# A planner's table of VectorE durations, and how far ahead steps of the head may stand

## The chip, the cores and the metric

The kernel runs on one core of a Trainium2 chip. The metric is the device time of one execution in microseconds (us). It has no loop on the chip: every instruction of the five engines is written out by a program that first makes a plan, and the plan alone fixes the order on each engine. TensorE is called PE here and in the rows, VectorE DVE, ScalarE ACT, GpSimd POOL, and SyncE, which issues the transfers, SP.

## What is computed

Sixteen sequences of 1024 tokens with 256 channels go through half a gated FFN, causal attention with 16 heads and rotary embedding, and the same FFN again, each on a layer norm without weights:

```
def ffn(x):                      # x_prev is x moved by one token, zero at the start
    xr = mu_r * x + (1 - mu_r) * x_prev
    xk = mu_k * x + (1 - mu_k) * x_prev
    r = sigmoid(xr @ W_r.T)
    return r * (square(relu(xk @ W_k.T)) @ W_v.T)

x = x + 0.5 * ffn(layernorm(x))
x = x + softmax(causal(rope(q) @ rope(k).T / 4)) @ v @ W_proj + b_proj    # q, k, v of layernorm(x)
x = x + 0.5 * ffn(layernorm(x))
```

## The kernel before

**Slots.** Time is cut into slots, one for each block of scores (`score_slot`). A score is one matmul of L938 (128 keys by up to 512 queries of one head), and 48 of them make up a group of four heads, so a batch has four groups and 192 slots; the whole program has 3072 scores. ACT takes the exponential of each score (L1064), and in bursts PE multiplies them with the values (L969). A slot has also a *maximum*: another matmul of queries by keys (L948), whose rows DVE reduces (L1175 for blocks on the diagonal, L1178 for the others) to the maxima that a later group's exponentials subtract. Three PSUM banks (`NM`) hold such blocks, so PE can't write the fourth before DVE has taken the first. The slots before the first of the second group's scores are the *head*: slot -120 is the start, the first 16 maxima stand from slot -53 (`HALF_MAX`), the others from -33 (`REST_MAX`), the first 16 scores (called S1 to S16 here) from -25, the 17th (S17) at slot 16. From there on the number of a slot and of its score agree.

**Background steps.** All else fills the gaps between scores and maxima: the FFN steps `f_...` of one chunk of 256 tokens (index p runs over 128 chunks in the order of `self.ffn`; p = 0 to 3 is batch 0, p = 4 to 7 batch 1), the layer norm and value steps `a_...`, the queries and keys `r_...`, the output projection `p_P`. On PE a background matmul of 128x256 in float32 is one of four of a step and shows as two records. The steps that matter here:

- `f_dif` on POOL (L1330) takes the difference to the token before. `f_k0`, `f_k1` on DVE (L1200) and `f_r0`, `f_r1` (L1206) make the mixed inputs from two SBUF tiles, `dif_sb` and `fxn_sb`. Then come `f_K` on PE (L1022), `f_R` (L1025), `f_V` (L1028), `f_u` on DVE (L1212, one operand in PSUM) and `f_xadd` on POOL (L1335).
- `r_QK` on PE (L1034), four transfers `r_swap` (L846), `r_cos` on POOL (L1348), `r_sin` and `r_add` on DVE (L1229, L1233, two SBUF tiles each), then `r_hi`, `r_rest`, `r_mid`, `r_low` split the result into three bfloat16 parts, and SP sends them to the rows that scores and maxima read (L861 for a whole group, `rows0` to `rows5`; L873 for the first half of the first group, `part0` to `part5`).
- `y_mul` on POOL (L1359), then `p_P` on PE (L1015) and `xp` on DVE.

**The planner.** `describe` gives each step a start slot t (`release`), and `step` turns it into the first slot in which it may stand. Two procedures place the steps. `place_early` handles the slots before 48 (`SWITCH`) by credits; it doesn't read the table of durations. From slot 48 on `place`, `fill` and `unit` keep a clock for each engine and read `TAKES`: name: (ns until the engine can begin the next instruction, ns until others see the result). A step is placed when its inputs are seen by that clock, and on DVE only where its first number fits before the next maximum.

Of the kernel before, what the change touches and what calls it, by code (L numbers as in the profile page):

```python
# [62 lines left out]
SWITCH = 48  # L63
# [22 lines left out]
class Plan:  # L86


    TAKES = {"f_st0": (335, 470), "f_st1": (600, 760), "f_rstd": (1600, 1700), "f_x0": (490, 645), "f_x1": (490, 645), "f_T": (440, 640),
             "f_xn": (477, 645), "f_dif": (1270, 1330), "f_k0": (397, 530), "f_k1": (397, 530), "f_r0": (397, 530), "f_r1": (397, 530),  # L90
             "f_relu": (477, 665), "f_sq": (500, 675), "f_tanh": (477, 645), "f_u": (600, 735), "f_xadd": (1222, 1330),
             "a_st0": (335, 470), "a_st1": (600, 760), "a_rstd": (1600, 1700), "a_x0": (490, 645), "a_x1": (490, 645), "a_T": (440, 640),
             "a_xn": (477, 645), "a_vc": (477, 645), "a_bias": (1222, 1330), "r_b0": (356, 530), "r_b1": (356, 530), "r_swap": (240, 7000),
             "r_cos": (1350, 1700), "r_sin": (700, 840), "r_add": (603, 740), "r_hi": (519, 680), "r_rest": (1170, 1500), "r_mid": (519, 680),
             "r_low": (1170, 1500), "store": (60, 5000), "load": (60, 7000), "h_fin": (700, 900), "h_T": (130, 400), "h_copy": (156, 330),
             "h_rows": (240, 2500), "m_fin": (900, 1000), "m_T": (130, 400), "m_copy": (157, 330), "m_rows": (60, 3000),
             "y_copy": (477, 645), "y_out": (120, 8000), "y_recip": (159, 300), "y_back": (60, 4500), "y_in": (120, 9000),
# [6 lines left out]
    HEARD_PE = 200  # L104
    UNIT = 4 * CH / GHZ
    TICK = 900
    EARLY = 60

    def __init__(self, nb):
        self.nb = nb  # L110
# [12 lines left out]
    def step(self, engine, name, i, cost, start, *after):  # L123

        turn = 0 if name[0] in "myh" else 1 if name[:4] in ("rows", "part") else 2
        early = start - self.EARLY if turn == 2 else start
        if name == "a_vc":
            early = max(early, (i // NCH - 1) * BSLOTS + PV_AT + 1)
        self.steps[name, i] = [engine, cost, (turn, start), early, [(n, k, lag) for n, k, lag in after if k >= 0]]
# [1288 lines left out]
```

## Time and profile before

| | us |
|---|---|
| median of 3 runs (3065.30 to 3073.12) | 3072.01 |
| the profiled execution | 3072.22 |
| its span, first to last instruction | 3070.50 |
| from the start to the first maximum's matmul | 89.18 |
| to S1 | 113.60 |
| to S17 | 158.90 |
| to the 49th, 97th, 145th, 193rd score | 190.79, 231.63, 272.61, 317.11 |
| two batches in the middle (192 scores each) | 181.60, 183.30 |

In the profile PE is busy for 95% of the span, DVE for 82%, ACT 72%, POOL 52%. In the first 100 us PE is busy for 66.77 us, from 100 to 200 us for 84.40. A busy PE isn't a PE at its peak, since the ends of matmuls are modelled. The chain that ended last runs over PE for 70% of the span and over DVE for 17%. The granted TensorE clock is 0.987 over the span.

### The profile page before, as it was taken

Reading aid. Unit: us, or ns where it says so; the run is one execution under the profiler, and the core shown is the slowest. Engines: PE = TensorE matmul, PEld = TensorE weight load, DVE = VectorE, ACT = ScalarE, POOL = GpSimd, SP = SyncE. Lnnn points to the kernel's source line nnn. Section 1 sums busy time; section 2 is a strip of 40 time slices with the busy share of each in tenths; the row PEclk is TensorE's granted clock in tenths of the full one; section 3 lists DMA queues with packets and bytes.
Section 4 is the critical chain, followed back from the end, with each engine's and each line's share of the span. In section 5 each row is a group of like instructions: output and inputs, shape, how many; then the busy total and the mean of one; then the engine's idle time right before and its main releaser. Section 6 shows DMA issues by size and latency. Waiting matters only on the chain.

```text
span 3070.5 us, 56204 instructions
## 1 busy us (share of the span) xinstructions
PE 2916.8 (95%) x18245; PEld 1710.7 (56%) x18245; DVE 2513.0 (82%) x7302; ACT 2197.9 (72%) x4802; POOL 1588.8 (52%) x2190
## 2 busy tenths in 40 slices
PE   6799999999999999999999999999999999999997
PEld 5545555655555555555555555565555655555444
DVE  3888888888888888888888888888888888888852
ACT  4467677777777777777777777777777777777663
POOL 5555544655555455555555555555455555555222
PEclk9899999999999999999999999999999999999998
DMA  3334443433433434443433433443343443443411
GB/s 100 67 67 78 77 94 68 97 78 74 95 73 86 84 74 90 79 98 60 101 78 71 92 77 88 81 88 77 75 105 60 98 78 71 95 79 86 78 44 35
DMA packets 202585, 245.49 MB, mean 80 GB/s; under 512 B 68405, under 2 KB 104245, under 8 KB 202293
## 3 DMA queue, kind: packets, MB, share of 16 engines
q1 hardware_dynamic: 202293, 241.90, 38.1%
q8 instruction: 146, 2.39, 0.4%
q14 instruction: 146, 1.20, 0.2%
HBM read 53.48 MB, written 51.38 MB: 34 GB/s over the span
## 4 chain that ended last, share of the span: by engine, by line
PE 70%; DVE 17%; issue 4%; ACT 4%; POOL 3%; DMA 1%; SPq 1%; POOLq 0%; DVEq 0%; ACTq 0%
PE ps_y L969 14%; PE ps_s L938 13%; PE ps_m L948 12%; PE ps_d L1022 7%; PE ps_d L1025 6%; PE ps_d L1028 5%; PE ps_d L1034 5%; DVE ps_m L1175 4%; DVE mx_sb L1178 3%; PE ps_d L1015 3%; PE ps_d L1038 3%; DVE ka_sb L1200 3%; PE ps_d L976 2%; ACT pt_sb L1064 2%; DVE dif_sb L1206 1%
## 5 line engine op out<-in xcount | busy, mean ns | idle before, releaser
L1064 ACT ACTIVATE pt_sb<-ps_s 128x512 f32<-128x512 f32 (+1 forms) x2532 | 1219.4, 492 | 483.7 <-PE ps_s L938 456.7
L1175 DVE CUSTOM_DVE_ANT_0 ps_m<-ps_m,mask_sb 128x128 f32<-128x128 f32 (+3 forms) x2048 | 993.1, 498 | 298.7 <-PE ps_m L948 282.5
L948 PE MATMUL ps_m<-kr_sb,qr_sb 96*128 96x512 bf16 (+3 forms) x3072 | 1002.3, 329 | 39.0 <-DVE mx_sb L1175 29.8
L938 PE MATMUL ps_s<-qr_sb,kr_sb 99*128 99x512 bf16 (+1 forms) x3039 | 996.5, 330 | 24.6 <-ACT pt_sb L1064 9.3
L1178 DVE TENSOR_REDUCE mx_sb<-ps_m 128x1 f32<-128x512 f32 x1024 | 699.0, 683 | 99.4 <-PE ps_m L948 92.3
L1307 POOL TENSOR_SCALAR_AFFINE_SELECT pt_sb<-pt_sb 128x512 f32<-128x512 f32 x384 | 255.6, 666 | 503.3 <-ACT pt_sb L1064 503.1
L948 PEld LDWEIGHTS ps_m<-kr_sb,qr_sb 96*128 96x128 bf16 x3072 | 301.9, 98 | 365.4 <-DVE mx_sb L1175 74.6
L969 PE MATMUL ps_y<-pt_sb,v_sb 128*32 128x512 f32 (+2 forms) x5120 | 494.5, 495 | 3.3 <-POOL pt_sb L1307 3.0
L938 PEld LDWEIGHTS ps_s<-qr_sb,kr_sb 99*128 99x128 bf16 x3039 | 293.4, 97 | 328.0 <-issue 134.0
L1064 ACT ACTIVATE pn_sb<-ps_s 128x384 f32<-128x384 f32 x507 | 244.7, 493 | 244.9 <-PE ps_s L938 243.4
L1022 PE MATMUL ps_d<-ka_sb,wk_sb 128*128 128x256 f32 x992 | 307.2, 398 | 29.4 <-DVE ka_sb L1200 28.7
L1025 PE MATMUL ps_d<-wr_sb,dif_sb 128*128 128x256 f32 x1024 | 307.5, 387 | 4.4 <-DVE dif_sb L1206 4.3
L1034 PE MATMUL ps_d<-axn_sb,wqk_sb 128*128 128x256 f32 x1024 | 305.3, 383 | 4.4 <-ACT axn_sb L1104 3.8
L1028 PE MATMUL ps_d<-wv_sb,ka_sb 128*128 128x256 f32 x992 | 296.4, 383 | 0.0
L1175 DVE DVE_READ_ACCUMULATOR2_ANT mx_sb<- 128x1 f32 x2048 | 285.9, 140 | 0.0
L969 PEld LDWEIGHTS ps_y<-pt_sb,v_sb 128*32 128x32 f32 x5120 | 141.6, 110 | 237.2 <-issue 210.6
L1335 POOL TENSOR_TENSOR x_sb<-x_sb,dif_sb 128x512 f32<-128x512 f32 x128 | 179.2, 1400 | 182.1 <-DVE dif_sb L1212 181.9
L1351 POOL TENSOR_TENSOR qb_sb<-qb_sb,part_sb 128x512 f32<-128x512 f32 x124 | 147.0, 1186 | 181.9 <-ACT part_sb L1123 181.6
L1022 PEld LDWEIGHTS ps_d<-ka_sb,wk_sb 128*128 128x128 f32 x992 | 178.2, 198 | 79.4 <-issue 40.1
L1034 PEld LDWEIGHTS ps_d<-axn_sb,wqk_sb 128*128 128x128 f32 x1024 | 180.6, 190 | 49.1 <-issue 3.7
L1200 DVE SCALAR_TENSOR_TENSOR ka_sb<-dif_sb,muk_sb,fxn_sb 128x256 f32<-128x256 f32 x248 | 200.5, 816 | 8.5 <-POOL dif_sb L1330 8.4
L1025 PEld LDWEIGHTS ps_d<-wr_sb,dif_sb 128*128 128x128 f32 x1024 | 178.9, 192 | 45.9 <-issue 6.7
(113 smaller groups left out, 3934.9 us busy)
## 6 DMA issues: line engine op xcount, KB each, us to landing
kr_sb<-part_sb SPq DMA_DIRECT2D x378, 128.0 KB, 4.5
qr_sb<-part_sb SPq DMA_DIRECT2D x378, 128.0 KB, 4.8
y_way<-yt_sb SPq DMA_DIRECT2D x128, 256.0 KB, 2.2
sw_sb<-qb_sb SPq DMA_DIRECT2D x496, 64.0 KB, 2.0
x_sb<-x SPq DMA_DIRECT2D x64, 256.0 KB, 3.9
yn_sb<-y_way SPq DMA_DIRECT2D x64, 256.0 KB
den_sb<-r_way SPq DMA_DIRECT2D x64, 256.0 KB
out<-x_sb SPq DMA_DIRECT2D x64, 256.0 KB, 2.4
```

Of the source, the lines that this page charges most:

```text
L938: eng.matmul(score_bank(slot)[:, 0:width], kr_sb[0:KR + NP, n % RS, j, kb * P:(kb + 1) * P], qr_sb[0:KR + NP, n % RS, j, q0:q0 + width], s ...
L948: eng.matmul(ps_m[:, u % NM, 0:width], qr_sb[0:KR, n % RS, j, i * P:(i + 1) * P], kr_sb[0:KR, n % RS, j, piece * QC:piece * QC + width], s ...
L969: pv_j = eng.matmul(ps_y[32 * j:32 * j + 32, QC - width:QC], v_sb[:, b % 2, kb, col:col + 32], buffer[:, j, column:column + width], start= ...
L1022: mm = eng.matmul(ps[:, rows], wk_sb[:, cc, cols], key_of(i)[:, cc, :], start=(cc == 0), stop=(cc == CC - 1))
L1025: mm = eng.matmul(ps[:, rows], dif_sb[:, i % 2, cc, cols], wr_sb[:, cc, :], start=(cc == 0), stop=(cc == CC - 1))
L1028: mm = eng.matmul(ps[:, rows], key_of(i)[:, cc, cols], wv_sb[:, cc, :], start=(cc == 0), stop=(cc == CC - 1))
L1034: mm = eng.matmul(ps[:, rows], wqk_sb[:, cc, w0:w0 + P], axn_sb[:, c, cc, :], start=(cc == 0), stop=(cc == CC - 1))
L1064: eng.activation(buffer[:, j, column:column + width], score_bank(slot)[:, 0:width], ACT.Exp, scale=SCALE).then_inc(exped, 1)
L1175: eng.tensor_tensor_reduce(ps_m[:, u % NM, 0:width], ps_m[:, u % NM, 0:width], mask_sb[:, m0:m0 + width], 1.0, -3e38, ALU.add, ALU.max, be ...
L1178: eng.tensor_reduce(best, ps_m[:, u % NM, 0:width], mybir.AxisListType.X, ALU.max).then_inc(max_taken, 1)
L1200: eng.scalar_tensor_tensor(out=key_of(i)[:, cc, :], in0=dif_sb[:, i % 2, cc, :], scalar=muk_sb[:, cc:cc + 1], in1=fxn_sb[:, i % 2, cc, 0:C ...
L1307: eng.affine_select(out=diag, in_=diag, compare_op=ALU.is_ge, fill=0.0, base=0, pattern=[[0, G], [1, P]], channel_multiplier=-1).then_inc( ...
```

## The change

```diff
     TAKES = {...
-             "f_xn": (477, 645), "f_dif": (1270, 1330), "f_k0": (397, 530), "f_k1": (397, 530), "f_r0": (397, 530), "f_r1": (397, 530),
+             "f_xn": (477, 645), "f_dif": (1270, 1330), "f_k0": (760, 900), "f_k1": (760, 900), "f_r0": (560, 700), "f_r1": (560, 700),
...
-             "r_cos": (1350, 1700), "r_sin": (700, 840), "r_add": (603, 740), "r_hi": (519, 680), "r_rest": (1170, 1500), "r_mid": (519, 680),
+             "r_cos": (1350, 1700), "r_sin": (820, 960), "r_add": (700, 840), "r_hi": (519, 680), "r_rest": (1170, 1500), "r_mid": (519, 680),
...
-    EARLY = 60
+    EARLY_HEAD, EARLY = 16, 60
...
-        early = start - self.EARLY if turn == 2 else start
+        early = min(start - self.EARLY_HEAD, max(start - self.EARLY, SWITCH)) if turn == 2 else start
```

No instruction is added, taken away or made different; instructions stand in another order. A background step (`turn == 2`) could stand up to 60 slots ahead of its start slot. Now a step whose start is before slot 64 may stand 16 ahead at most, one with a start between 64 and 108 not before slot 48, and later ones 60 ahead as before. The six names in the table are the DVE steps with two SBUF operands; the table acts from slot 48 on.

**The head, on PE**, from the projections of batch 0's last chunks to the first maxima (L1034 queries and keys, L1038 values, L976 a transpose, L1007 the bias, L1022, L1025 and L1028 the FFN of batch 1's first chunk). Before:

```order
25 L1034 MATMUL ps_d<-axn_sb,wqk_sb 128x256 x4
26 L1038 MATMUL ps_d<-wvv_sb,axn_sb 128x256 x8
27 L1034 MATMUL ps_d<-axn_sb,wqk_sb 128x256 x8
28 L976 MATMUL ps_d<-id_sb,dif_sb 128x128 x4
29 L1007 MATMUL ps_d<-wp_sb,yt_sb 128x256 x2
30 L1022 MATMUL ps_d<-ka_sb,wk_sb 128x256 x4
31 L1025 MATMUL ps_d<-wr_sb,dif_sb 128x256 x4
32 L1028 MATMUL ps_d<-wv_sb,ka_sb 128x256 x4
33 L948 MATMUL ps_m<-kr_sb,qr_sb 128x512 x2
34 L1034 MATMUL ps_d<-axn_sb,wqk_sb 128x256 x3
```

Now:

```order
25 L1034 MATMUL ps_d<-axn_sb,wqk_sb 128x256 x4
26 L1038 MATMUL ps_d<-wvv_sb,axn_sb 128x256 x8
27 L948 MATMUL ps_m<-kr_sb,qr_sb 128x512 x4
28 L948 MATMUL ps_m<-kr_sb,qr_sb 128x128 x4
29 L948 MATMUL ps_m<-kr_sb,qr_sb 128x384 x4
30 L948 MATMUL ps_m<-kr_sb,qr_sb 128x256 x4
31 L1034 MATMUL ps_d<-axn_sb,wqk_sb 128x256 x4
32 L997 MATMUL ps_d<-idb_sb,hp_sb 48x128
```

The 22 background matmuls and the transpose between the values and the first maximum stand later; the first sixteen maxima follow each other.

**Behind the head, on PE**, around the 103rd to 106th score, where work arrives that stood in the head. Before:

```order
378 L938 MATMUL ps_s<-qr_sb,kr_sb 128x384
379 L948 MATMUL ps_m<-kr_sb,qr_sb 128x256
380 L938 MATMUL ps_s<-qr_sb,kr_sb 128x384
381 L948 MATMUL ps_m<-kr_sb,qr_sb 128x512
382 L938 MATMUL ps_s<-qr_sb,kr_sb 128x256
383 L948 MATMUL ps_m<-kr_sb,qr_sb 128x256
```

Now:

```order
379 L938 MATMUL ps_s<-qr_sb,kr_sb 128x384
380 L948 MATMUL ps_m<-kr_sb,qr_sb 128x256
381 L1038 MATMUL ps_d<-wvv_sb,axn_sb 128x256
382 L938 MATMUL ps_s<-qr_sb,kr_sb 128x384
383 L948 MATMUL ps_m<-kr_sb,qr_sb 128x512
384 L1022 MATMUL ps_d<-ka_sb,wk_sb 128x256
385 L938 MATMUL ps_s<-qr_sb,kr_sb 128x256
386 L948 MATMUL ps_m<-kr_sb,qr_sb 128x256
387 L1022 MATMUL ps_d<-ka_sb,wk_sb 128x256
```

Each slot has a background matmul now where it had none.

**In the middle of the run, on DVE**, around the 1061st score. Before:

```order
2571 L1200 SCALAR_TENSOR_TENSOR ka_sb<-dif_sb,muk_sb,fxn_sb 128x256
2572 L1175 ISA ps_m,mx_sb<-ps_m,mask_sb 128x384
2573 L1175 ISA mx_sb 128x1
2574 L1175 ISA ps_m,mx_sb<-ps_m,mask_sb 128x256
2575 L1175 ISA mx_sb 128x1
2576 L1229 TENSOR_TENSOR sw_sb<-sw_sb,sin_sb 128x512
2577 L1200 SCALAR_TENSOR_TENSOR ka_sb<-dif_sb,muk_sb,fxn_sb 128x256
2578 L1233 TENSOR_TENSOR qb_sb<-qb_sb,sw_sb 128x512
2579 L1206 SCALAR_TENSOR_TENSOR dif_sb<-dif_sb,mur_sb,fxn_sb 128x256 x2
2580 L1175 ISA ps_m,mx_sb<-ps_m,mask_sb 128x256
```

Now:

```order
2570 L1175 ISA ps_m,mx_sb<-ps_m,mask_sb 128x384
2571 L1175 ISA mx_sb 128x1
2572 L1175 ISA ps_m,mx_sb<-ps_m,mask_sb 128x256
2573 L1175 ISA mx_sb 128x1
2574 L1200 SCALAR_TENSOR_TENSOR ka_sb<-dif_sb,muk_sb,fxn_sb 128x256 x2
2575 L1206 SCALAR_TENSOR_TENSOR dif_sb<-dif_sb,mur_sb,fxn_sb 128x256
2576 L1175 ISA ps_m,mx_sb<-ps_m,mask_sb 128x256
2577 L1175 ISA mx_sb 128x1
2578 L1206 SCALAR_TENSOR_TENSOR dif_sb<-dif_sb,mur_sb,fxn_sb 128x256
```

Five steps stood between two maxima; now there are three, and the rotary steps aren't in this gap.

## Rows read from the trace of the kernel before

**Rows 1.** The page: busy us (share of the span) xinstructions of each engine.

```profile
PE 2916.8 (95%) x18245; PEld 1710.7 (56%) x18245; DVE 2513.0 (82%) x7302; ACT 2197.9 (72%) x4802; POOL 1588.8 (52%) x2190
```

**Rows 2.** Waits of PE from 576 to 2640 us: us in total, times, longest.

```profile
PE ps_m L948 <- DVE mx_sb L1175: 13.6, 17, 1.0
PE ps_d L1022 <- DVE ka_sb L1200: 12.5, 16, 1.1
PE ps_d L1015 <- POOL yn_sb L1359: 9.0, 11, 1.5
PE ps_d L1025 <- DVE dif_sb L1206: 4.3, 11, 0.5
```

**Rows 3.** DVE's groups by form: xcount | busy us, mean ns | idle before, releaser.

```profile
L1178 DVE TENSOR_REDUCE mx_sb<-ps_m 128x1 f32<-128x512 f32 x1024 | 699.0, 683 | 99.4 <-PE ps_m L948 92.3
...
L1200 DVE SCALAR_TENSOR_TENSOR ka_sb<-dif_sb,muk_sb,fxn_sb 128x256 f32<-128x256 f32 x248 | 200.5, 816 | 8.5 <-POOL dif_sb L1330 8.4
L1206 DVE SCALAR_TENSOR_TENSOR dif_sb<-dif_sb,mur_sb,fxn_sb 128x256 f32<-128x256 f32 x256 | 152.9, 610 | 0.0
...
L1229 DVE TENSOR_TENSOR sw_sb<-sw_sb,sin_sb 128x512 f32<-128x512 f32 x124 | 110.7, 892 | 8.5 <-DMA sw_sb<-qb_sb 8.5
...
L1233 DVE TENSOR_TENSOR qb_sb<-qb_sb,sw_sb 128x512 f32<-128x512 f32 x124 | 95.2, 768 | 4.9 <-POOL qb_sb L1348 3.2
```

**Rows 4.** Timeline of DVE around the 1061st score: start us, us, instruction.

```profile
1138.57 1.46 DVE L1200 SCALAR_TENSOR_TENSOR ka_sb<-dif_sb,muk_sb,fxn_sb 128x256 f32<-128x256 f32 x1
...
1140.81 0.91 DVE L1229 TENSOR_TENSOR sw_sb<-sw_sb,sin_sb 128x512 f32<-128x512 f32 x1
...
1142.42 1.76 DVE L1233 TENSOR_TENSOR qb_sb<-qb_sb,sw_sb 128x512 f32<-128x512 f32 x1
1144.11 0.87 DVE L1206 SCALAR_TENSOR_TENSOR dif_sb<-dif_sb,mur_sb,fxn_sb 128x256 f32<-128x256 f32 x2
```

**Rows 5.** Timeline of POOL in the same stretch.

```profile
1142.19 1.44 POOL L1335 TENSOR_TENSOR x_sb<-x_sb,dif_sb 128x512 f32<-128x512 f32 x1
```

**Rows 6.** Timeline of PE right behind it.

```profile
1145.43 0.39 PE L948 MATMUL ps_m<-kr_sb,qr_sb 96*128 96x512 bf16 x1 [1.01 <-DVE mx_sb L1175]
```

**Rows 7.** Timeline of PE in the head.

```profile
61.96 3.62 PE L1038 MATMUL ps_d<-wvv_sb,axn_sb 128*128 128x256 f32 x16
...
81.27 3.75 PE L1022 MATMUL ps_d<-ka_sb,wk_sb 128*128 128x256 f32 x8 [4.94 <-DVE ka_sb L1200]
...
89.18 0.60 PE L948 MATMUL ps_m<-kr_sb,qr_sb 96*128 96x512 bf16 x2
```

**Rows 8.** Timeline of DVE in the head.

```profile
70.13 0.69 DVE L1233 TENSOR_TENSOR yn_sb<-yn_sb 128x512 f32<-128x512 f32 x1 [1.16 <-POOL yn_sb L1348]
...
101.54 0.84 DVE L1249 TENSOR_SCALAR hp_sb<-mx_sb 128x16 bf16<-128x16 f32 x1
```

**Rows 9.** Timeline of SP in the head: the last `part` transfer and the last of `rows5`.

```profile
59.39 0.59 SPq L873 DMA_DIRECT2D qr_sb<-part_sb  x1
...
84.07 0.59 SPq L861 DMA_DIRECT2D qr_sb<-part_sb  x1
```

**Rows 10.** The page's transfers: xcount, KB each, median us from issue to landing.

```profile
kr_sb<-part_sb SPq DMA_DIRECT2D x378, 128.0 KB, 4.5
```

**Rows 11.** Two stretches, of L938 alone: us, PE busy (xscores), PEld busy, clock, DMA, GB/s.

```profile
89.18:113.60 24.42, 0.00 (x0) 0.10 (x1) 0.93 0.17 43
113.60:158.90 45.30, 4.99 (x16) 1.57 (x16) 0.89 0.46 70
```

**Rows 12.** Stretches of 48 scores, of `ps_d` alone: us, PE busy (xrecords), PEld, DVE, ACT, clock.

```profile
231.63:272.61 40.98, 13.74 (x51) 8.40 (x51) 0.68 (x1) 4.29 (x9) 1.00 0.45 77
...
407.30:453.60 46.30, 26.46 (x96) 15.72 (x95) 1.35 (x2) 7.40 (x14) 1.00 0.49 98
...
634.30:678.50 44.20, 22.31 (x84) 13.28 (x83) 1.35 (x2) 6.32 (x12) 1.00 0.43 79
2828.50:2861.70 33.20, 0.22 (x1) 0.12 (x1) 0.00 (x0) 0.45 (x2) 1.00 0.47 82
```

## The prediction

> **What bounds the kernel now.** I read the page first, then the waits of PE in the middle of the run, then the lines and the timeline of DVE, last the head. PE is busy for 95% of the span and DVE for 82% [rows 1]: PE is the bound through most of the run, with DVE close behind. The work is fixed, so a new order can win only what PE waits for, and what the head loses before the first scores. In the middle, over 2064 us, PE waits 13.6 us for a maximum's bank that DVE hasn't freed, 12.5 us for `f_k`, 4.3 us for `f_r` and 9.0 us for `y_mul` [rows 2]. That is 39 us in about eleven batches: the ceiling for the middle.
>
> The causes are in DVE's rows. A step of L1200 takes 816 ns on the mean where the planner reckons with 397, one of L1206 610 (397), L1229 892 (700), L1233 768 (603) [rows 3]. Consecutive DVE records overlap a little, so the new entries, 760, 560, 820 and 700, are near the mean pace. But the mean hides two kinds. One step of L1200 took 1.46 us [rows 4]. In the pile of five steps that the last excerpt of the order shows, L1233 took 1.76 us while POOL ran L1335, and two steps of L1206 behind it took 0.87 us together [rows 4, 5]. By the old table this pile takes 2.5 us (700 + 397 + 603 + 2 x 397 ns); by the trace it lasts from 1140.81 to about 1144.9, 4.1 us [rows 4]. PE then waited 1.01 us for the bank [rows 6].
>
> **The head: first maxima and first scores.** Until PE has made the values, which end at 61.96 + 3.62 = 65.6 us [rows 7], its order is the same. Before, 22 background matmuls stood ahead of the first maximum. Twelve are the FFN of batch 1's first chunk, and PE waited 4.94 us for their `f_k` alone; the first maximum came at 89.18 [rows 7]. The rows it reads were not the cause: their last transfer was issued at 59.39 [rows 9] and takes some 4.5 us [rows 10], so they lay there at 64.5. Now PE can make it at 65.6, and DVE, after `r_add` of the last chunk (70.13 + 0.69 [rows 8]), takes it at 70.8. The sixteen first maxima took from 89.18 to 101.54 with other steps between [rows 7, 8], 12.4 us, so at most as long now: done by 83.2. The next maxima need the whole group's rows. Their last transfer was issued at 84.07 [rows 9]; with 0.59 us of issue and 4.5 to land that is 89.2. Now no `load` and no `r_swap` stands between these issues, and ACT and POOL no longer have batch 1's FFN between the parts of the last chunk. I take 4 us for it: 85. Eight maxima at some 0.76 us (683 ns by L1178 [rows 3]; diagonal ones take a little more) and one `r_sin` of 0.9 bring S1 to about 91.5, where it stood at 113.60 [rows 11]. **Gain 22 us**; 18 if the rows land as late as before; 24 at best.
>
> From S1 to S17, 45.30 us [rows 11], the order holds 33 background matmuls both times, and 25 DVE steps for 24: **0**. From S17 to the 49th score it holds 20 for 16, and 13 DVE steps for 6. Seven steps of 0.6 to 0.9 us are 5 us if DVE binds there, 1.8 us of matmuls if PE does: **cost 3.5 us**.
>
> **Behind the head: what was moved comes back.** Up to the 49th score, 33 fewer background matmuls are done; from there to the 145th score there are now 73 for 41, and by the 193rd both orders are level within one matmul. A background matmul is two records of 0.226 us (3.62 us for 16 [rows 7]), 0.45 us, if PE has no room. It has some: a stretch of 48 scores with 51 records took 40.98 us and one with 96 took 46.30 us at the same place of a batch, 5.3 us for 45 records, 0.24 us for each background matmul [rows 12]. 32 matmuls cost 7.7 us at that price and 14.4 us at the full one. Eleven more DVE steps come with them where DVE has little room, so I take **9 us**.
>
> From the 193rd to the 577th score the new order has 22 fewer (277 for 299), at 0.24 us a **gain of 5 us**. They come back between scores 2689 and 2881 (148 for 128). Sixteen of them fill a stretch that had none; it took 33.20 us with one record, and the like stretch with 84 took 44.20 [rows 12], 0.13 us a record, so 4.2 us, and 1 us for the rest: **cost 5 us**. The last chunks behind the last score stand as before: 0.
>
> Sum outside the middle: -22 + 0 + 3.5 + 9 - 5 + 5 = **-9.5 us**.
>
> **The middle, eleven batches.** The new table makes piles smaller: no gap has more than four steps where six were possible. In the gap shown, three steps remain for five. Of 13.6 us for banks I let two thirds go: -9. The projection stood one slot behind its `y_mul` in two of eight cases and stands ten slots or more behind in all of them now: -9 [rows 2]. `f_R` has fewer close followers: -2 of 4.3. `f_K` is the weak place: before, it stood in the slot right behind `f_k1` in 5 of 16 cases, now in 8. The planner has more time in that slot, but a step beside POOL takes twice what it has: 0 of 12.5. Last, one more slot in each batch has no background matmul at all, at about 0.25 us: +3. The sum is **-17 us**; bounds are -36 (all of rows 2, less 3) and +15 (`f_K`'s waits grow with its close followers and with POOL, and nothing else goes).
>
> The profiled execution took 3072.2 us around its span of 3070.5, as the median of 3072.0. 3072.2 - 9.5 - 17 = 3045.7: I predict **3046 us**.
>
> **A rule of the skill.** L1206 ran at 0.44 us each with POOL out of the way, and L1233 took 1.76 us beside L1335 [rows 4, 5]. The Trainium skill, SBUF — State Buffer, "Who interferes with whom", says that a VectorE instruction with two SBUF inputs contends with a GpSimd instruction that reads SBUF. The trace agrees. By that rule no single number is right for these steps, which speaks against this change; it is the first rival.
>
> **Rivals.** *Slower: the new order makes more steps meet POOL.* `f_k0` follows `f_dif` on POOL at once, and POOL's next step starts then too. Eight of 16 `f_K` stand in the slot behind `f_k1`, 64 in the run. A pair that meets POOL takes up to twice 1.46 us [rows 4], where the table has 1.5 for both: 1.4 us late. If half of these 64 meet it, that is 45 us for `f_K`, less 12.5 that is already paid, and longer DVE steps eat the gain on the other waits. Then the middle costs some 30 us: 3072.2 - 9.5 + 30 = **3093 us**. It decides once more than about a third of the close pairs meet POOL. For it: in the mean of L1200, 816 ns, (816 - 440)/(1460 - 440), some four steps in ten are slow already. Against it: the steps that met POOL now cost only 12.5 us.
>
> *The same: the head's gain is paid back in full.* The first maxima wait for the group's rows as before (-18), the moved matmuls cost 0.45 us each behind the head (32 at 14.4 us, after the 5 us of DVE steps before them), the late ones cost 9 (20 at 0.45) where 5 are gained ahead, and the middle gives 2: 3072.2 - 18 + 5 + 14.4 - 5 + 9 - 2 = **3076 us**. For it: PE is at 95%, and work moved out of a stretch where it idles must be done where it doesn't.
>
> *Faster still:* all waits of rows 2 but the 3 us of empty slots go, and S1 comes at 89.5: 3072.2 - 11.5 - 36 = **3025 us**.
>
> *The change doesn't do what it says* in the head: the procedure that places the head doesn't read the table, and the limit of sixteen slots could bind on nothing. The order excludes this; 66 steps leave the head.
>
> **How the numbers follow.** A measurement can tell about 0.3% (9 us) from no change. Chances: forecast (3034 to 3055) 0.42, faster still 0.18, the same 0.23, slower 0.17. "Faster by over 0.3%" is under 3062.8: the first two and a little of the third, 0.63; within 0.3% 0.21; slower 0.16. The range takes in the bounds of the middle with the head's at their likely values, and leaves out the far part of the slower rival: 3019 to 3082.
>
> **What would show it.** Right if S1 stands at 89 to 95 us, S17 at 134 to 141, the 49th score near 172 and the 193rd near 307 (317.11 before), and if two batches in the middle take about 363 us for 366. The wait of L1015 for `y_mul` should be gone, that of L948 for DVE a third. Wrong if the first maximum still comes after 75 us, if the 193rd score is no earlier than before, or if the mean of L1200 rises well above 816 ns and the wait of L1022 doubles.

## The result, and the profile of the changed kernel

The change makes the kernel slower: 3113.70 us (median of 4 runs, 3111.85 to 3117.54) against 3070.81 us (4 runs, 3065.30 to 3073.12), a ratio of 1.0138 with an interval of 1.0124 to 1.0153. The prediction of 3046 us (range 3019 to 3082) is wrong, in its sign too: it put PE's wait for the row transfers at nothing, and that wait is 83.3 us. The profiled execution has a span of 3111.9 us, 41.4 more than before.

The start of each numbered score or maximum, read from the timeline of PE (us):

| | before | after | difference |
|---|---|---|---|
| first maximum | 89.18 | 64.30 | -24.9 |
| S1 | 113.60 | 87.8 | -25.8 |
| S17 | 158.90 | 138.8 | -20.1 |
| 49th score | 190.79 | 171.7 | -19.1 |
| 97th | 231.63 | 214.6 | -17.0 |
| 145th | 272.61 | 274.7 | +2.1 |
| 193rd | 317.11 | 317.7 | +0.6 |
| 577th | 678.5 | 665.4 | -13.1 |
| 2689th | 2691.0 | 2731.4 | +40.3 |
| 2881st | 2861.7 | 2914.7 | +53.0 |
| the last | 3008.1 | 3052.7 | +44.5 |

So the head came as forecast, and the middle went the other way: 53.4 us lost in eleven batches where 17 were to be won. The page answers [rows 1]; PE, DVE, ACT and POOL are each busy within 7.5 us of what they were:

```profile
PE 2924.2 (94%) x18245; PEld 1722.0 (55%) x18245; DVE 2507.9 (81%) x7302; ACT 2200.9 (71%) x4802; POOL 1581.4 (51%) x2190
```

The waits of PE from 576 to 2700 us answer [rows 2] (what is waited for: us in total, times, longest):

```profile
PE ps_m L948 <- DMA qr_sb<-part_sb: 65.6, 11, 6.9
PE ps_s L938 <- ACT pt_sb L1064: 10.7, 33, 0.5
PE ps_d L1025 <- DVE dif_sb L1206: 0.2, 1, 0.2
```

All four waits that the prediction counted are gone, three of them whole. A wait that the rows of before don't have has taken their place: the maximum's matmul waits for the transfer of the rows it reads, once in each batch from the fifth on (batches are counted from 0, so 4 to 15), and once in batch 1. Over the whole run it is

```profile
PE ps_m L948 <- DMA qr_sb<-part_sb: 83.3, 13, 12.3
```

Twelve of these stand at the first maximum of a batch's first group (groups 16, 20, ... 60; group 4b is the first of batch b) and take 5.1 to 6.9 us each; one of 12.3 us stands at group 4. In the timeline of PE (start us, us, instruction, idle before) the one at group 24:

```profile
1163.44 0.38 PE L938 MATMUL ps_s<-qr_sb,kr_sb 99*128 99x512 bf16 x1
1170.05 0.61 PE L948 MATMUL ps_m<-kr_sb,qr_sb 96*128 96x512 bf16 x1 [6.23 <-DMA qr_sb<-part_sb]
1170.45 1.06 PE L1038 MATMUL ps_d<-wvv_sb,axn_sb 128*128 128x256 f32 x2
```

and SP's timeline just ahead of it:

```profile
1154.84 0.65 SPq L838 DMA_DIRECT2D out<-x_sb  x1
1155.58 0.61 SPq L891 DMA_DIRECT2D dcol_sb<-yt_sb  x1
1156.23 0.50 SPq L892 DMA_DIRECT2D y_way<-yt_sb  x1
1156.77 0.56 SPq L861 DMA_DIRECT2D kr_sb<-part_sb  x1
1157.38 0.60 SPq L861 DMA_DIRECT2D qr_sb<-part_sb  x1
1158.15 0.65 SPq L906 DMA_DIRECT2D yn_sb<-y_way  x1
1158.85 0.64 SPq L909 DMA_DIRECT2D den_sb<-r_way  x1
1159.53 0.61 SPq L861 DMA_DIRECT2D kr_sb<-part_sb  x1
1160.18 0.61 SPq L861 DMA_DIRECT2D qr_sb<-part_sb  x1
```

The last row transfer is issued at 1160.18. Before, that transfer of the same group was issued at 1154.24 for a maximum at 1168.65. Landing takes longer too. Minimum, median and maximum from issue to landing of the row transfers (L861), for all twelve of this group before, and for the last five that write `qr_sb` now:

```profile
DMA to landing us min/median/max: 3.4/4.4/5.7
DMA to landing us min/median/max: 4.6/5.0/9.8
```

The 9.8 is that of the last one: 1160.18 + 9.8 = 1170.0, where the matmul starts.

VectorE's two-operand steps answer [rows 3] (count, busy us, mean ns, idle before):

```profile
L1200 DVE SCALAR_TENSOR_TENSOR ka_sb<-dif_sb,muk_sb,fxn_sb 128x256 f32<-128x256 f32 x248 | 182.3, 746 | 5.7 <-POOL dif_sb L1330 5.7
L1206 DVE SCALAR_TENSOR_TENSOR dif_sb<-dif_sb,mur_sb,fxn_sb 128x256 f32<-128x256 f32 x256 | 151.9, 602 | 0.0
...
L1229 DVE TENSOR_TENSOR sw_sb<-sw_sb,sin_sb 128x512 f32<-128x512 f32 x124 | 122.0, 984 | 5.0 <-DMA sw_sb<-qb_sb 5.0
...
L1233 DVE TENSOR_TENSOR qb_sb<-qb_sb,sw_sb 128x512 f32<-128x512 f32 x124 | 97.4, 785 | 13.5 <-POOL qb_sb L1348 10.9
```

The mean of L1200 fell from 816 to 746 ns and that of L1229 rose from 892 to 984. The busy time of the four is 553.6 us for 559.3.

### The profile page after: what moved, and what is told of

The parts are those of the page before. It is cut to its first block, busy times and chain, and to the rows that moved or that the text cites. A ratio compares the mean times of both kernels' runs of the same rounds, so it can differ in the third digit from the quotient of the medians.

```text
span 3111.9 us, 56208 instructions
## 1 busy us (share of the span) xinstructions
PE 2924.2 (94%) x18245; PEld 1722.0 (55%) x18245; DVE 2507.9 (81%) x7302; ACT 2200.9 (71%) x4802; POOL 1581.4 (51%) x2190
## 4 chain that ended last, share of the span: by engine, by line
PE 76%; DVE 8%; SPq 6%; DMA 5%; ACT 3%; issue 2%; POOL 1%; POOLq 0%; DVEq 0%; ACTq 0%
PE ps_y L969 15%; PE ps_s L938 14%; PE ps_m L948 13%; PE ps_d L1025 7%; PE ps_d L1034 6%; PE ps_d L1028 6%; PE ps_d L1022 6%; DMA qr_sb<-part_sb 4%; PE ps_d L1015 3%; SPq L861 3%; DVE ps_m L1175 3%; PE ps_d L1038 3%; PE ps_d L976 3%; DVE mx_sb L1178 2%; ACT pt_sb L1064 2%
## 5 line engine op out<-in xcount | busy, mean ns | idle before, releaser
L948 PE MATMUL ps_m<-kr_sb,qr_sb 96*128 96x512 bf16 (+3 forms) x3072 | 1014.2, 332 | 114.8 <-DMA qr_sb<-part_sb 83.3
L938 PE MATMUL ps_s<-qr_sb,kr_sb 99*128 99x512 bf16 (+1 forms) x3039 | 1003.6, 331 | 28.3 <-ACT pt_sb L1064 17.7
L938 PEld LDWEIGHTS ps_s<-qr_sb,kr_sb 99*128 99x128 bf16 x3039 | 294.9, 97 | 341.8 <-issue 135.6
L1025 PE MATMUL ps_d<-wr_sb,dif_sb 128*128 128x256 f32 x1024 | 319.3, 399 | 0.6 <-DVE dif_sb L1206 0.6
L1034 PE MATMUL ps_d<-axn_sb,wqk_sb 128*128 128x256 f32 x1024 | 314.2, 392 | 3.8 <-ACT axn_sb L1104 3.8
L1022 PE MATMUL ps_d<-ka_sb,wk_sb 128*128 128x256 f32 x992 | 301.9, 388 | 8.5 <-DVE ka_sb L1200 7.8
L1028 PE MATMUL ps_d<-wv_sb,ka_sb 128*128 128x256 f32 x992 | 297.7, 384 | 0.0
L1335 POOL TENSOR_TENSOR x_sb<-x_sb,dif_sb 128x512 f32<-128x512 f32 x128 | 171.3, 1338 | 101.4 <-DVE dif_sb L1212 100.9
L1025 PEld LDWEIGHTS ps_d<-wr_sb,dif_sb 128*128 128x128 f32 x1024 | 188.3, 201 | 44.2 <-issue 10.0
L1307 POOL TENSOR_SCALAR_AFFINE_SELECT pn_sb<-pn_sb 128x512 f32<-128x512 f32 x128 | 82.0, 640 | 254.5 <-ACT pn_sb L1064 254.5
L1034 PEld LDWEIGHTS ps_d<-axn_sb,wqk_sb 128*128 128x128 f32 x1024 | 178.9, 194 | 46.9 <-issue 3.9
L1022 PEld LDWEIGHTS ps_d<-ka_sb,wk_sb 128*128 128x128 f32 x992 | 172.3, 193 | 57.3 <-issue 9.6
```

The costliest lines, as they stand in the source:

```text
L938: eng.matmul(score_bank(slot)[:, 0:width], kr_sb[0:KR + NP, n % RS, j, kb * P:(kb + 1) * P], qr_sb[0:KR + NP, n % RS, j, q0:q0 + width], s ...
L948: eng.matmul(ps_m[:, u % NM, 0:width], qr_sb[0:KR, n % RS, j, i * P:(i + 1) * P], kr_sb[0:KR, n % RS, j, piece * QC:piece * QC + width], s ...
L1022: mm = eng.matmul(ps[:, rows], wk_sb[:, cc, cols], key_of(i)[:, cc, :], start=(cc == 0), stop=(cc == CC - 1))
L1025: mm = eng.matmul(ps[:, rows], dif_sb[:, i % 2, cc, cols], wr_sb[:, cc, :], start=(cc == 0), stop=(cc == CC - 1))
L1028: mm = eng.matmul(ps[:, rows], key_of(i)[:, cc, cols], wv_sb[:, cc, :], start=(cc == 0), stop=(cc == CC - 1))
L1034: mm = eng.matmul(ps[:, rows], wqk_sb[:, cc, w0:w0 + P], axn_sb[:, c, cc, :], start=(cc == 0), stop=(cc == CC - 1))
```

## The experiments

**The theory.** The new table makes the planner place the background chain of a batch later: layer norm, queries and keys, rotary steps, row transfers. By the plans, the last of the row steps (`rows5`) stood 15 slots ahead of the first maximum of each batch's first group, and from group 16 on it now stands 5 ahead; the `r_low` that it sends stood 34 ahead and now 12. The 5 slots don't cover issue and landing, and PE waits. The head's limit does the same to group 4 alone. **The rivals:** the loss is the price of the work moved out of the head (*paid back*), or VectorE's steps meet POOL more often (*POOL*). "Rows ahead" below is the distance in the plan from `rows5` to that maximum, at group 4 and at groups 16, 20, ... 60 (middle); the wait is that of PE for `qr_sb<-part_sb` at the first maxima of the groups, without single waits under 0.9 us; the batch is the mean of ten batches between the 577th and the 2497th score.

| kernel | rows ahead, group 4 / middle | waits, us (times) | a batch, us | median, us |
|---|---|---|---|---|
| before | 15 / 15 | 0 | 183.1 | 3071 to 3074 |
| changed | 4 / 5 | 83.3 (13) | 187.8 | 3113.7 |
| table alone | 15 / 5 | 70.8 (12) | 187.6 | 3115.2 |
| head alone | 1 / 15 | 10.6 (1) | 183.1 | 3070.3 |
| rotary entries old | 4 / 15 | 12.5 (1) | 181.3 | 3040.2 |
| rows issued earlier (than planned) | 4 / 5 | 12.0 (1) | 181.7 | 3041.1 |
| margin 1000 | 4 / 12 | 11.5 (1) | 180.2 | 3026.2 |
| slack 500 | 11 / 15 | 3.9 (1) | 181.5 | 3043.7 |
| rotary entries alone | 1 / 1 | 109.6 (14) | 191.8 | 3171.2 |
| rows issued earlier, limit 28 | 12 / 5 | 0.9 (1) | 181.7 | 3035.1 |
| margin 1000, limit 28 | 12 / 12 | 0 | 180.2 | 3024.1 |
| margin 1000, limit at the first maximum | 15 / 12 | 0 | 180.2 | 3018.9 |
| old table, limit 28 | 15 / 15 | 0 | 183.2 | 3071.7 |
| old table, margin 1000 | 15 / 12, but 8 at group 28 and 1 at group 32 | 11.7 (2) | 184.7 | 3106.5 |

**The two halves apart.** The table alone:

```diff
-        early = min(start - self.EARLY_HEAD, max(start - self.EARLY, SWITCH)) if turn == 2 else start
+        early = start - self.EARLY if turn == 2 else start
```

> The table alone; the head stands as before the change. Theory 'late rows': the new table puts the row transfers of each batch's first group only 5 slots ahead of the maximum that reads them (15 before), so twelve waits of about 6.2 us for them (groups 16 to 60) stay, each followed by some 5 us at half the TensorE clock; group 4 has its rows 15 slots ahead, so its wait of 12.3 us is not there, and neither is the head's gain of 19 us. From the 49th score to the 577th it should run as before the change (488 us), from there as the changed kernel. That gives 3113.7 + 19 - 12.3 - 2 + 11 or so: 3120 to 3132 us, and waits of L948 for the rows of some 71 us in all. Rival 'paid back' (the loss is the price of the work moved out of the head): 3050 to 3065, since nothing is moved. Rival 'POOL' (the new order makes VectorE's two-operand steps meet GpSimd): 3110 to 3130 as well, but with the loss in waits of PE for DVE, not for the rows.

Measured: 3115.24 us, ratio 1.0139 [1.0120, 1.0159]; twelve waits, 70.8 us, none at group 4, as expected. The time is 5 us under the 3120 to 3132 expected: from the 49th to the 577th score it takes 473.5 us, where the 487.7 of before had been reckoned with. The head alone is the kernel before with

```diff
-        early = start - self.EARLY if turn == 2 else start
+        early = min(start - 16, max(start - self.EARLY, SWITCH)) if turn == 2 else start
```

> The sixteen-slot limit alone, with the old table. Late rows: in the middle the rows stand 15 slots ahead again, so no wait for them there and 183 us for a batch as before; at group 4 they stand 1 slot ahead (4 in the changed kernel), so that wait is 12 to 18 us. Against the kernel before: -19 us at the 49th score, about +22 to the 145th, -10 to the 577th, then level: 3060 to 3070 us. Rival 'paid back': 3105 to 3115, with the loss spread over the run. Rival 'POOL': about 3050 to 3060, and nothing in it speaks for the table's part.

Measured: 3070.34 us, ratio 0.9989 [0.9978, 1.0001]. The expectation was 3060 to 3070, with a wait of 12 to 18 us at group 4; it is 10.6. So the whole loss is the table's, and it lies in the waits. The rival *paid back* doesn't make the loss, but with the old table it holds for the head: 19.0 us ahead at the 49th score, 0.4 behind at the 577th, 10.6 of it in the wait at group 4.

**The cause itself.** In the changed kernel only SP's order is edited; the orders of PE, DVE, ACT and POOL are word for word the same:

```diff
-            for slot in slots:
-                for name, i in plan.at["SP"].get(slot, ()):
+            line = [step for slot in slots for step in plan.at["SP"].get(slot, ())]
+            for g in range(NG, nb * NG, NG):
+                for k in (4, 5):
+                    line.remove((f"rows{k}", g))
+                    line.insert(line.index((f"rows{k - 1}", g)) + 1, (f"rows{k}", g))
+            if True:
+                for name, i in line:
```

> The changed kernel with every order as it is but SP's: from group 4 on, the last two of the six row steps of each batch's first group are issued right behind the fourth, ahead of a store and the transfers of the attention's result that stood between. The orders of PE, DVE, ACT and POOL are the changed kernel's, word for word. Late rows: the last row transfer is issued some 3.4 us earlier and has fewer transfers ahead of it in the queue, so the wait of 6.2 us falls to 0 to 3 us, and with it most of the 5 us at half clock: 3113.7 less 40 to 95 us, 3020 to 3075. Rivals 'POOL' and 'paid back': no VectorE, GpSimd or TensorE instruction stands elsewhere, so 3105 to 3120.

Measured: 3041.08 us, ratio to the kernel before 0.9900 [0.9882, 0.9918]; 73 us less than the changed kernel. SP's timeline at the same place (line numbers from here on are 5 higher in this kernel: L866 is L861):

```profile
1145.61 0.60 SPq L866 DMA_DIRECT2D kr_sb<-part_sb  x1
1146.25 0.59 SPq L866 DMA_DIRECT2D qr_sb<-part_sb  x1
1146.89 0.59 SPq L843 DMA_DIRECT2D out<-x_sb  x1
1147.58 0.61 SPq L896 DMA_DIRECT2D dcol_sb<-yt_sb  x1
1148.23 0.49 SPq L897 DMA_DIRECT2D y_way<-yt_sb  x1
1148.88 1.00 SPq L911 DMA_DIRECT2D yn_sb<-y_way  x1
```

the row transfers' landing there, the maximum, which doesn't wait, and PE's waits from 576 to 2700 us:

```profile
DMA to landing us min/median/max: 3.4/5.3/6.3
```

```profile
1153.24 0.38 PE L953 MATMUL ps_m<-kr_sb,qr_sb 96*128 96x512 bf16 x1
```

```profile
PE ps_s L943 <- ACT pt_sb L1069: 11.6, 36, 0.5
PE ps_m L953 <- DVE mx_sb L1180: 10.9, 13, 1.6
PE ps_m L953 <- DVE mx_sb L1183: 3.4, 11, 0.3
PE ps_m L953 <- DMA qr_sb<-part_sb: 1.1, 2, 0.9
```

The store and the transfers of the attention's result, four of them of 256 KB, now stand behind the last rows. From the end of `r_low` to the last issue it takes 6.1 us (1140.17 to 1146.25) where it took 9.6 (1150.58 to 1160.18), and the slowest landing 6.3 for 9.8: 7 us in all, for a wait of 6.2. This settles the cause. Not one instruction of VectorE or GpSimd stands elsewhere, which leaves neither rival for these waits.

**The same by way of the plan.** Rotary entries old:

```diff
-             "r_cos": (1350, 1700), "r_sin": (820, 960), "r_add": (700, 840), "r_hi": (519, 680), "r_rest": (1170, 1500), "r_mid": (519, 680),
+             "r_cos": (1350, 1700), "r_sin": (700, 840), "r_add": (603, 740), "r_hi": (519, 680), "r_rest": (1170, 1500), "r_mid": (519, 680),
```

> The changed kernel with r_sin and r_add at their old entries (700, 840 and 603, 740); f_k and f_r keep the new ones. Late rows: in this plan the rows of the middle groups stand 15 slots ahead of their maxima, those of group 4 still 4. So 12 waits of L948 for rows go (71 us, and some 2.5 us behind each at half clock), the one of 12.3 us at group 4 stays: 3113.7 - 71 - 30 = about 3013 if nothing else moves, 3010 to 3050 with the waits for DVE that may come back. Rival 'POOL': f_k and f_r are 504 of the 752 steps with a new entry and keep it, so most of the loss stays: 3090 to 3115.

Measured: 3040.20 us, ratio 0.9894 [0.9878, 0.9911]; only group 4's wait is left. The reverse is the changed kernel with

```diff
-             "f_xn": (477, 645), "f_dif": (1270, 1330), "f_k0": (760, 900), "f_k1": (760, 900), "f_r0": (560, 700), "f_r1": (560, 700),
+             "f_xn": (477, 645), "f_dif": (1270, 1330), "f_k0": (397, 530), "f_k1": (397, 530), "f_r0": (397, 530), "f_r1": (397, 530),
```

> The changed kernel with f_k and f_r at their old entries, r_sin and r_add at the new ones: by the plan the row steps stand only 1 slot ahead of their maxima at group 4 and at the middle groups, the last part (r_low) 1 slot. Late rows, as a dose the other way: a wait of about 12 us at each of the thirteen groups (4 slots ahead cost 12.3 at group 4, 5 ahead 6.2 in the middle; r_low to maximum took 19.5 us with 5 slots ahead, some 10 to 12 of it the row steps and their landing), so 160 us of waits: 3160 to 3230. Rival 'POOL': fewer steps have new entries and the piles are more as before the change, so 3060 to 3115.

Measured: 3171.15 us (2 runs), ratio 1.0321 [1.0300, 1.0342]. So the two rotary entries by themselves are what makes the rows late, 1 slot ahead of the maximum; with the entries of `f_k` and `f_r` added it is 5. The waits are 7.6 to 9.4 us in the middle, not the 12 expected: at group 24 it took 13.5 us from the end of `r_low` to the maximum, where it took 19.5 in the changed kernel, and the slowest row transfer landed after 8.3 us for 9.8. The direction was right, the size of a wait per slot was not.

The planner's margin for SP, which it adds to a step's inputs, 1000 for 1500 ns:

```diff
-    MARGIN = {"PE": 0, "ACT": 200, "DVE": 400, "POOL": 400, "SP": 1500}
+    MARGIN = {"PE": 0, "ACT": 200, "DVE": 400, "POOL": 400, "SP": 1000}
```

> The changed kernel with the planner's margin for SP at 1000 ns instead of 1500: the row steps of each batch's first group stand 12 slots ahead of their maximum in the middle (5 in the changed kernel, 15 before the change), at group 4 still 4. Late rows, as a dose: 7 slots of some 0.95 us are 6.6 us, just the wait, so 0 to 1.5 us of it remain at each of the twelve groups; group 4 keeps its 12 us. With the undisturbed pace seen where the rows were issued earlier (181.75 us for 192 scores): 3040, 3030 to 3055. Rival 'POOL', or anything else in the order of VectorE: the new table is unchanged, so 3095 to 3120.

Measured: 3026.19 us, ratio 0.9850 [0.9835, 0.9865], below the 3030 to 3055 expected. Twelve slots are enough. The margin gives more than the rows' wait: the eleven batches from the 577th to the 2689th score take 1981.5 us, 18 less than with the rows issued earlier, and only 6 of these are waits of PE (19.4 us of all kinds for 25.3). The rest was not taken further. And VectorE's slack, how far past the next maximum a step's first number may reach:

```diff
-    SLACK = {"ACT": 250, "DVE": 400, "POOL": 1300, "SP": 300}
+    SLACK = {"ACT": 250, "DVE": 500, "POOL": 1300, "SP": 300}
```

> The changed kernel with all new entries and VectorE's slack (how far past the next maximum a step's first number may reach) at 500 ns instead of 400: rows 15 slots ahead in the middle, 11 at group 4. Late rows: no wait in the middle, 0 to 3 us at group 4: 3025, 3015 to 3045. Rival 'POOL': the six entries stand, VectorE's steps only may reach 100 ns further: 3095 to 3115.

Measured: 3043.65 us, ratio 0.9903 [0.9886, 0.9921]; the middle as expected (rows 15 slots ahead with all six new entries, and no wait), the whole at the upper end: from the 193rd to the 577th score it takes 362.2 us where the changed kernel takes 347.7.

**Group 4 and the head.** In the kernel with the rows issued earlier, the limit at 28:

```diff
-    EARLY_HEAD, EARLY = 16, 60
+    EARLY_HEAD, EARLY = 28, 60
```

> The changed kernel with the last two row steps issued earlier on SP (3041 us with that alone) and, besides, 28 for 16 as the number of slots that a step of the head may stand ahead. The order of PE up to the first maxima is the changed kernel's, so the first scores come as early; group 4's rows stand 12 slots ahead of its first maximum for 4. Late rows: the wait of 12 us at group 4 goes, the rest stays: 3029, 3022 to 3036. Rival 'paid back' (the head's gain is lost to the matmuls that come back, not to that wait): 3038 to 3048.

Measured: 3035.06 us, ratio 0.9875 [0.9859, 0.9890]. The wait of 12 us goes and 6 us of the median come (12.1 of the span); the scores start later, S1 at 95.9 us for 90.2. The result lies at the upper end of the first expectation, and short of the rival's. Up to the 577th score, where neither kernel waits for rows, it is 4.6 us ahead of the table alone (658.4 for 663.0): with the new table and this limit, some of the head's gain stays. Margin and limit together, in the changed kernel:

```diff
-    EARLY_HEAD, EARLY = 16, 60
+    EARLY_HEAD, EARLY = 28, 60
...
-    MARGIN = {"PE": 0, "ACT": 200, "DVE": 400, "POOL": 400, "SP": 1500}
+    MARGIN = {"PE": 0, "ACT": 200, "DVE": 400, "POOL": 400, "SP": 1000}
```

> The changed kernel with SP's margin at 1000 ns (3026 us with that alone) and 28 for 16 in the head: rows 12 slots ahead in the middle and 12 at group 4. The 11.5 us wait at group 4 goes; where the same step to 28 was made with the row steps issued earlier, the span fell by 12.1 us and the median by 6. So 3017, 3012 to 3023. If the two don't add up (the head's gain was already spent): 3024 to 3029.

Measured: 3024.10 us, ratio 0.9841 [0.9824, 0.9859]: 2.1 us less than with the margin alone by the median, 6 us by the span, and at the lower edge of the 3024 to 3029 that were expected if the two don't add up. That they add up isn't shown. The old table with a limit of 28, on the kernel before:

```diff
-        early = start - self.EARLY if turn == 2 else start
+        early = min(start - 28, max(start - self.EARLY, SWITCH)) if turn == 2 else start
```

> The kernel before with the old table and a limit of 28 slots in the head. With 16 slots and the old table the head's 19 us were gone at the 577th score (3070.3 us against 3071.0), 10.6 of them in the wait at group 4. Here group 4's rows stand 15 slots ahead. Late rows: that wait isn't there and some 10 us of the head's gain stay: 3060, 3055 to 3064. Rival 'paid back': the moved matmuls eat it whatever the rows do, 3067 to 3073.

Measured: 3071.65 us, ratio 0.9994 [0.9984, 1.0003]. This is the time that *paid back* expected (3067 to 3073): no wait for rows, and still nothing is left of the head. It goes between the 97th and the 145th score, 51.2 us where the same limit with the new table and the margin takes 41.5. PE waits for DVE there, which first stood for a transfer and then ran the five steps of `m_fin` (timelines of DVE and of PE):

```profile
255.76 0.25 DVE L1276 RECIPROCAL dcol_sb<-dcol_sb 128x16 f32<-128x16 f32 x1 [2.07 <-DMA dcol_sb<-yt_sb]
...
257.44 1.10 DVE L1267 SCALAR_TENSOR_TENSOR mres_sb<-mx_sb,mp_sb 128x32 f32<-128x32 f32 x1
258.57 1.18 DVE L1270 CAST mp_sb<-mres_sb 128x32 bf16<-128x32 f32 x1
...
259.89 0.69 DVE L1175 CUSTOM_DVE_ANT_0 ps_m<-ps_m,mask_sb 128x512 f32<-128x512 f32 x1
```

```profile
260.70 0.61 PE L948 MATMUL ps_m<-kr_sb,qr_sb 96*128 96x512 bf16 x1 [6.13 <-DVE mx_sb L1175]
```

The four steps from L1261 to L1270 took 0.57 to 1.18 us each, 3.7 in all, where their means over this run are 0.20 to 0.42; POOL ran four instructions without a gap from 255.51 to 259.71. So this limit loses in another place what the limit of 16 lost at the rows.

**A version that beats both kernels.** The new table, SP's margin at 1000, and in the head

```diff
-        early = min(start - self.EARLY_HEAD, max(start - self.EARLY, SWITCH)) if turn == 2 else start
+        early = min(start - self.EARLY_HEAD, max(start - self.EARLY, HALF_MAX)) if turn == 2 else start
```

> The changed kernel with SP's margin at 1000 ns, and in the head a step may stand as far ahead as the slot of the first maximum (60 slots at most) where it had to stay behind slot 48 or within 16 slots. Nothing of batch 1 stands before the first maxima, 74 background units stand between them and S17 (41 in the changed kernel, 56 before), group 4's rows are 15 slots ahead or more. First maximum at 64 us, S17 at 148 to 155, no wait at group 4. If matmuls in the head cost less there than later (PE has room): 3012 to 3020; if each delays the scores at its full price: 3020 to 3028. I take 3017.

Measured: 3018.88 us, ratio 0.9823 [0.9806, 0.9840], the fastest here. S17 comes at 151.3 us, 12.5 later than in the changed kernel, yet the 145th score at 261.3 for 274.7.

**The margin without the table**, the kernel before with

```diff
-    MARGIN = {"PE": 0, "ACT": 200, "DVE": 400, "POOL": 400, "SP": 1500}
+    MARGIN = {"PE": 0, "ACT": 200, "DVE": 400, "POOL": 400, "SP": 1000}
```

> The kernel before with SP's margin at 1000 ns and nothing else: the new table and the head's limit are not in it. It tells what of the 3026 us is the table's. If the table is worth what the prediction had for the middle, two batches stay at 366 us here and the whole at 3066 to 3075. If the margin did it: 3035 to 3050.

Measured: 3106.53 us, ratio 1.0112 [1.0092, 1.0133], outside both expectations. PE waits for the rows twice, at group 28 (1.0 us) and at group 32 (10.6 us), where by the plan they stand 8 slots and 1 slot ahead; and DVE frees the maxima's banks late, 37.3 us where it was 13.6 [rows 2] (waits of PE, 576 to 2700 us):

```profile
PE ps_m L948 <- DVE mx_sb L1175: 37.3, 61, 1.6
PE ps_m L948 <- DMA qr_sb<-part_sb: 11.7, 2, 10.6
```

With the same margin, the new table and the head's limit at 16 it was 11.8 us for these banks and 3026 us in all. Of the 80 us between the two little should be the head's, which with the old table and the margin of 1500 moved the median by 0.7 us; at this margin it wasn't tried apart. So the table is worth a lot in one plan and costs 44 us in another. Why the old table does so badly at this margin was not taken further.

## Why the prediction was wrong, point by point

**The head, -22 us: right, a little low.** S1 came at 87.8 for 91.5 (the prediction's own terms add up to 92.0). PE made the first maximum at 64.30, right behind the values, and DVE took it behind `r_add` (timeline of PE, then of DVE):

```profile
60.85 3.62 PE L1038 MATMUL ps_d<-wvv_sb,axn_sb 128*128 128x256 f32 x16
64.30 0.81 PE L948 MATMUL ps_m<-kr_sb,qr_sb 96*128 96x512 bf16 x3
```

```profile
68.74 1.62 DVE L1233 TENSOR_TENSOR yn_sb<-yn_sb 128x512 f32<-128x512 f32 x1 [2.27 <-POOL yn_sb L1348]
70.29 0.69 DVE L1175 CUSTOM_DVE_ANT_0 ps_m<-ps_m,mask_sb 128x512 f32<-128x512 f32 x1
...
77.80 0.18 DVE L1249 TENSOR_SCALAR hp_sb<-mx_sb 128x16 bf16<-128x16 f32 x1
```

The sixteen took 7.5 us on DVE (70.29 to 77.80), where 12.4 were allowed, since no other step stands between them. The group's rows were there at 81.4 (85 forecast): their last transfer was issued at 79.02 and landed after 2.4 us, where 4.5 had been reckoned with.

**S1 to S17, 0: it cost 5.7 us.** 51.0 us for 45.30, with 33 background matmuls as before. The stretches of [rows 11] in the changed kernel, of L938 alone (us, PE busy, PEld busy, clock, DMA share, GB/s):

```profile
64.30:87.80 23.50, 0.03 (x1) 0.03 (x1) 0.71 0.17 51
87.80:138.80 51.00, 5.02 (x17) 1.68 (x17) 0.80 0.40 68
```

The granted clock is 0.71 and 0.80 where it was 0.93 and 0.89: with the background work gone from between the first maxima, PE is busy for 14.74 of the first 23.50 us, where it was for 18.05 of 24.42. From S1 to S17 it is busy for 38.88 us (35.94 before) and waits 11.6 us for the maxima's banks (7.7 before). That the lower clock is what costs the 5.7 us wasn't tested apart.

**S17 to the 49th, +3.5: 32.9 us for 31.9, +1.0. The 49th to the 145th, +9: +21.2,** of which 12.3 are the wait at group 4. The other 8.9 fit the forecast term; no run with this limit goes without the wait, but with the slack at 500, where it is 3.9 us, the rest is 9.5. What was missed is the wait, by its kind: the 32 moved matmuls were priced as time on PE, and the prediction didn't ask who needs what they make.

**The 193rd to the 577th, -5, and the late scores, +5: the order already showed a sign of the error here.** The order showed 22 fewer background matmuls in the first stretch and 20 more in the second. The windows of `ps_d` (us, PE busy with its records, PEld, DVE, ACT, clock, DMA share, GB/s), of after:

```profile
317.70:665.40 347.70, 179.02 (x643) 105.88 (x642) 14.46 (x22) 48.12 (x92) 1.00 0.44 86
2731.40:2914.70 183.30, 96.52 (x340) 56.87 (x340) 7.49 (x11) 25.28 (x48) 0.98 0.40 74
```

and of before:

```profile
317.11:678.50 361.39, 194.25 (x694) 115.12 (x694) 14.81 (x22) 50.22 (x96) 0.99 0.43 83
2691.00:2861.70 170.70, 81.65 (x288) 47.77 (x288) 6.78 (x10) 21.33 (x41) 1.00 0.40 79
```

51 fewer records gave 13.7 us, 52 more took 12.6 (5.3 of it the wait at group 60); 8.5 came back from the 2881st score to the last, and 3.1 behind it, where 0 was forecast. The sizes were off: in the first stretch PE is busy for 339.2 us instead of 351.0, which is 0.46 us for each of the 25.5 matmuls and not 0.24. The reading failed too: from the 193rd score to the 2689th the chain *lags* by these matmuls, and the prediction booked that as a loan of 5 us to be paid back at the end. The head has no part in it. The table alone takes 349.0 us for this stretch, with 649 records, and the head alone 362.0, with 701. The lag is the whole chain's: `r_QK` of the last chunk of group 24's queries and keys stood 61 slots ahead of the maximum, and stands 36 ahead now. What makes it lag is the room that a rotary step asks for on DVE: with the old rotary entries, or with 100 ns more slack, it stands 56 ahead.

**The middle, -17 us: -12.2 us without the new wait, +53.4 with it. Here is the step that failed.** The sum has a term for each wait that [rows 2] show and none for the wait for `qr_sb<-part_sb`, which was put at nothing without a reason; it is 65.6 us in these eleven batches, and 83.3 in the whole run. The kernel with the rows issued earlier has the same orders and not the wait, so the terms are read there. It takes 1999.8 us for these eleven batches, 12.7 less than before; two batches take 363.5 us, where 363 were forecast. The single terms are less good than their sum. L1015's wait is gone (-9.0, as forecast), `f_R`'s too (-4.1 for -2), and `f_K`'s is gone as well, 12.5 us [rows 2] where nothing was forecast. The banks gave nothing: 10.9 + 3.4 = 14.3 us, 13.6 before [rows 2], where -9 was forecast; and PE waits 11.6 us for ACT's exponentials, where it waited 6.0, of which the prediction had no term. In the changed kernel those waits are gone only because DVE catches up while PE waits for the rows. The bound of +15 on the slow side was too small by its making. It held only waits that the trace of before shows, grown or shrunk, while a distance that is covered shows no wait at all: 15 slots there, 5 now. The order of the changed kernel shows the distance, and the prediction read it for PE's matmuls and for `y_mul`, and not for the maxima behind the row transfers.

**The rivals.** *More steps meet POOL* gave the sign and a time 21 us off, by a mechanism that didn't happen: the mean of L1200 fell, and the wait of L1022 is gone in the middle. *Paid back in full* is right for the head with the old table, and was right in what speaks for it: neither limit left anything of the 15 to 18 us it had at S17. *The signs of being wrong* were well chosen only in part: the 193rd score was no earlier (317.7), and none of them looked at a wait that before doesn't have.

## What to carry to other kernels

When a change moves work later, follow it to whoever reads it: for each thing that is made late, take the distance to its first reader in the order of before and of after, and hold it against issue and landing, transfers above all. A wait that is zero in the profile may be covered by a hair or by far, and only the distance tells which. A table that describes an engine better can still make a plan worse, when the other entries leave no room for it. Here a row step has 240 ns in the table and is two issues of 0.6 us each, so six of them are 1.4 us in the plan and 7.2 in the trace; no run changed that entry.

## What the runs showed of the hardware

Behind a wait of 6.2 us PE works at half its clock for some 5 us. Windows of the changed kernel (us, then PE, PEld, DVE, ACT and POOL busy, clock, DMA share, GB/s):

```profile
1163.80:1170.00 6.20, 0.01 (x1) 0.00 (x0) 0.27 (x3) 1.11 (x2) 2.88 (x3) 0.89 0.74 140
1170.00:1175.00 5.00, 4.95 (x12) 2.92 (x13) 2.97 (x9) 1.68 (x3) 0.13 (x1) 0.50 0.05 13
1175.00:1180.00 5.00, 5.00 (x31) 2.39 (x30) 3.35 (x7) 2.44 (x5) 2.32 (x2) 0.96 0.04 8
```

0.50 is the 1.2 GHz level: 12 matmul records in 5 us, then 31. I had expected some 2.5 us more for each wait from this, about 30 us in all. In the batch it doesn't show: that fell from 187.8 to 181.7 us when the wait went, 6.1 us for the wait's own 6.0 (65.6/11). But PE's order is the same in both kernels, so their timelines can be laid side by side. Twelve matmuls behind the maximum the changed kernel is a further 2.0 to 2.5 us late at each of the eleven groups, 25.6 in all, and sixty matmuls behind it only 5.3 of these are left. So the price was paid and given back: in the other kernel PE waits for DVE in that time (14.3 us for the maxima's banks in eleven batches, none in the changed one). The windows of the eleven batches, changed kernel first, then the one with the rows issued earlier (us, PE, PEld, DVE, ACT, POOL busy, clock, DMA share, GB/s):

```profile
665.41:2731.35 2065.94, 1981.20 (x12540) 1176.96 (x12541) 1731.27 (x5017) 1511.84 (x3303) 1083.97 (x1498) 0.98 0.42 81
669.05:2668.88 1999.83, 1965.09 (x12541) 1164.75 (x12541) 1734.24 (x5017) 1509.22 (x3303) 1081.53 (x1498) 1.00 0.43 83
```

PE is busy for 16.1 us less and idle for 50.0 less, 66.1 in all.

At group 24 a transfer of 128 KB landed after 6.3 us at most where the 256 KB ones stood behind it, and after 9.8 where they stood ahead of it; at group 4 it took up to 11.8 us, with `yn_sb`, `den_sb` and `y_way` issued just before. The median over the whole run, 4.5 us [rows 10], told nothing of the one that is waited for; in that same run the longest took 9.4. The Trainium skill, DMA: Bandwidth & Descriptors, "Two DMAs through the same engine are not ordered", says that within one queue of one DMA engine descriptors start in order but are pipelined, and that nothing orders transfers across the 16 engines. No view here shows where a descriptor starts. The landings agree as far as they go: what stood ahead was paid for, and yet two `sw_sb` transfers that SP issued 0.7 and 1.3 us behind the last row transfer of group 24 landed 4.5 and 3.4 us before it (1165.51 and 1166.59 for 1170.00).
